# A mixture of experts in two parts of padded rows, with its results summed by TensorE through diagonal matrices

## The reference, cut to what matters

```python
logits = xt @ router_w.T                      # xt: 4096 x 128, router_w: 8 x 128
topk_vals, topk_idx = jax.lax.top_k(logits, 2)
g = jax.nn.sigmoid(topk_vals)
g = g / (g.sum(axis=-1, keepdims=True) + 1e-10)
# every chosen expert e of a token: (silu(x @ w_gate[e]) * (x @ w_up[e])) @ w_down[e]
```

## Time and profile before

| what | value |
|---|---|
| median of three runs | 2016.98 us (2016.55 to 2017.09) |
| the profiled execution | 2013.99 us |
| its span, first to last instruction | 2012.2 us |
| PE, DVE, ACT, POOL busy, share of the span | 85%, 76%, 68%, 44% |
| mean granted clock of TensorE | 0.923 |
| start of the mixture of experts | about 1727 us |

### The profile page before, as it was taken

How to read it: one execution, slowest core, us unless ns; L and a number is a source line. 1 busy time by engine, 2 the same in 40 slices (tenths; PEclk the granted TensorE clock), 3 DMA queues, 4 the chain that set the end, 5 groups by cost and what they waited for, 6 DMA issues and landing times. The chain is left out here.

```text
span 2012.2 us, 39279 instructions
## 1 busy us (share of the span) xinstructions
PE 1715.0 (85%) x12410; PEld 1129.4 (56%) x12410; DVE 1527.1 (76%) x4148; ACT 1360.3 (68%) x4708; POOL 883.9 (44%) x824
## 2 busy tenths in 40 slices
PE   4999999999999974899999696899999696744991
PEld 2555555555555542677777453677777453543660
DVE  2898898988889875899999455799999484753445
ACT  2888888888888854688888432688888455322555
POOL 3555565555565544333333123233333153385554
PEclk9999999999999985899999898899999898655996
DMA  6990000000000000000000110000000110012225
GB/s 201 214 179 2 2 2 2 2 1 2 1 2 1 2 1 6 6 17 17 12 17 12 26 32 7 6 17 16 13 17 12 26 32 2 8 46 70 82 64 135
DMA packets 102525, 65.90 MB, mean 33 GB/s; under 512 B 27698, under 2 KB 93874, under 8 KB 102322
## 3 DMA queue, kind: packets, MB, share of 16 engines
q1 hardware_dynamic: 97970, 54.40, 12.6%
q0 software_dynamic: 4352, 8.99, 1.3%
HBM read 19.50 MB, written 30.24 MB: 25 GB/s over the span
## 5 line engine op out<-in xcount | busy, mean ns | idle before, releaser
L216 POOL TENSOR_SCALAR a_aT<-a_dT 128x384 f32<-128x384 f32 x256 | 309.4, 1208 | 299.1 <-PE a_psO L529 187.5
L411 ACT ACTIVATE a_E<-a_psS,a_nm 128x128 f32<-128x128 f32 (+1 forms) x1028 | 418.8, 428 | 31.3 <-DVE a_nm L245 28.9
L245 DVE TENSOR_REDUCE a_nm<-a_psS 128x2 f32<-128x256 f32 (+1 forms) x514 | 260.1, 547 | 43.6 <-PE a_psS L496 42.9
L492 PE MATMUL a_psS<-a_kT,a_qm 32*128 32x128 f32 (+1 forms) x2064 | 240.6, 351 | 5.6 <-issue 3.6
L270 DVE SCALAR_TENSOR_TENSOR a_d<-a_E,a_cf 128x128 f32<-128x128 f32 (+1 forms) x512 | 219.3, 468 | 27.9 <-DVE a_cf L259 1.4
L411 ACT ACTIVATION_READ_ACCUMULATOR a_E<-a_psS,a_nm 128x1 f32 x1028 | 219.8, 214 | 0.0
L788 POOL TENSOR_TENSOR b0rn<-b0ss,minus_half 128x16 f32<-128x16 f32 x36 | 107.1, 2976 | 224.0 <-DVE b0ss L824 224.0
L788 POOL TENSOR_TENSOR b1rn<-b1ss,minus_half 128x16 f32<-128x16 f32 x36 | 107.1, 2976 | 221.5 <-DVE b1ss L824 221.5
L420 ACT ACTIVATE a_dT<-a_psT 128x384 f32<-128x384 f32 x256 | 126.7, 495 | 74.3 <-PE a_psT L505 71.3
L492 PEld LDWEIGHTS a_psS<-a_kT,a_qm 32*128 32x128 f32 x2064 | 136.6, 186 | 55.8 <-issue 35.5
L505 PE MATMUL a_psT<-ident,a_d 128*128 128x128 f32 x768 | 132.4, 281 | 6.2 <-DVE a_d L270 0.3
(11 more groups left out here) (353 smaller groups left out, 4411.9 us busy)
## 6 DMA issues: line engine op xcount, KB each, us to landing
mx_rows<-mx_blank SPq DMA_DIRECT2D x9, 2080.0 KB, 27.4
mx_xin<-mx_rows SPq DMA_DIRECT2D x72, 65.0 KB
b0v<-b0v SPq DMA_DIRECT2D x34, 128.0 KB, 2.3
b1v<-b1v SPq DMA_DIRECT2D x34, 128.0 KB
F<-mx_results SPq DMA_DIRECT2D x8, 256.0 KB, 5.2
mx_second<-mx_results SPq DMA_DIRECT2D x8, 256.0 KB, 5.4
out_dram<-X SPq DMA_DIRECT2D x8, 256.0 KB, 2.3
f0z<-F SPq DMA_DIRECT2D x9, 128.0 KB
```

Of the source, the lines that this page charges most:

```text
L216: pool.tensor_scalar(aT[:, s, :], dT[:, s, :], 0.0, None, ALU.max).then_inc(positived.sem, 1)
L245: ins = dve.tensor_reduce(nm[:, s, t, :], psS[:, s, :, (0, P)[t]:(P, 384)[t]], axis=AX.X, op=ALU.max, negate=True)
L411: ins = act.activation(E[:, s, m, c0:c1], psS[:, s, m, c0:c1], ACT.Exp, bias=nm[:, s, t, m:m + 1], accum_out=Z[:, p, h, t, m:m + 1])
L492: pe.matmul(psS[:, s, m, c0:c1], qm[rows, p, a, r, t * P:(t + 1) * P], kT[rows, p, a, 0:c1 - c0], start=(t == 0), stop=False)
```

## The change

- The groups are in two parts: groups 0 to 4 are the first, groups 5 to 7 the second. Each part has table regions, counts and a list of its own. Since each part needs up to eight half-filled tiles, there are 48 + 32 = 80 slots instead of 72.
- The slots of the first part start when its own sends are done. The last 12 sends (half of group 6 and all of group 7) are put one by one between the slots' scatters on POOL. The last group's routing, ranks and list lie between slots on PE and DVE: `route(7)` at slot 1, `choose(7)` at slot 3, `ranks(7)` at slot 6, `place(7)` at slot 8, the second list at slots 10 to 14.
- A row of the table has 144 numbers instead of 130. The ring of results `y` has 8 buffers instead of 4. `psH` has one bank instead of two, and the router's and the ranks' results share one bank.
- At the end ACT's and DVE's weighting is gone. DVE makes, for every tile, two diagonal matrices `ident * sg` (`spread`), those of the first part between slots 18 and 37, those of the second during the end. PE multiplies each tile's two results by them and sums both in PSUM. Statistics and norm read that PSUM tile; DVE adds the residual instead of POOL.

```diff
-ROW = D + 2
+ROW = D + 16
-SLOTS = 2 * TILES + NE
+FIRST = (0, 5, GROUPS)
+PART_TILES = [NT * (FIRST[p + 1] - FIRST[p]) for p in range(2)]
+PART_SLOTS = [2 * n + NE for n in PART_TILES]
+START = [0, PART_SLOTS[0], sum(PART_SLOTS)]
+SLOTS = START[2]
...
+                    if i == START[part]:
+                        sp.wait_ge(sent[part], 16 * 2 * PART_TILES[part])
...
+                    load(i)
+                    if i == START[1] + RING + 2:
+                        fetch(0)
+            fetch(1)
...
+            def spread(t):
+                dve.tensor_scalar(firsts[:, t, :], ident[:, :], sg[:, t, 0:1], None, ALU.mult)
+                dve.tensor_scalar(seconds[:, t, :], ident[:, :], sg[:, t, 1:2], None, ALU.mult).then_inc(diagonal, 1)
...
+            gates(0)
+            choose(LATE - 1)
+            place(LATE - 1)
+            outer.shifts(dve, LATE)
...
+            for g in range(GROUPS + 2):
                 if g < GROUPS:
-                    dve.wait_ge(weighted, g + 1)
...
                     dve.wait_ge(summed, g + 1)
                     ln.statistics(dve, g)
-                if g >= 1:
+                if 1 <= g <= GROUPS:
                     ln.shifts(dve, g - 1)
+                if g >= 2:
+                    dve.wait_ge(normal, g - 1)
+                    dve.tensor_tensor(ln.tiles(X, g - 2), ln.tiles(X, g - 2), second[:, of(g - 2), :], ALU.add)\
+                       .then_inc(done, 1)
+                if g == 0:
+                    gates(1)
...
+                if 1 <= g <= GROUPS - FIRST[1]:
+                    for t in range(NT):
+                        spread(NT * (FIRST[1] + g - 1) + t)
...
+            for g in range(GROUPS):
+                ln.apply(act, g, second[:, of(g), :]).then_inc(normal, 1)
...
+            pe.wait_ge(y_ready, SLOTS)
+            for g in range(GROUPS):
+                pe.wait_ge(diagonal, NT * (g + 1))
+                pe.wait_ge(fetched[g], 32)
+                if g >= 2:
+                    pe.wait_ge(normal, g - 1)
+                for t in range(NT):
+                    z = psY[:, g % 2, t * P:(t + 1) * P]
+                    pe.matmul(z, firsts[:, g * NT + t, :], ln.tiles(F, g)[:, t, :], start=True, stop=False)
+                    ins = pe.matmul(z, seconds[:, g * NT + t, :], second[:, g * NT + t, :], start=False, stop=True)
+                ins.then_inc(summed, 1)
```

More of the change, by code:

```diff
@@ L1589, in mixture_of_experts @@
         fetched = [sem(f"fetched{g}") for g in range(GROUPS)]
-        weighted, summed, normal, done, stored = (sem(n) for n in ("weighted", "summed", "normal", "done", "stored"))
+        diagonal, summed, normal, done, stored = (sem(n) for n in ("diagonal", "summed", "normal", "done", "stored"))
+        ln.sums = psY
         block = ctx.enter_context(nc.Block())
@@ L1604, in _ @@
         def _(sp):
[L1605 to L1617, removed]
@@ L1619, in _, with load @@
-            for k in range(4):
-                sp.wait_ge(scattered[k], 16 * (SLOTS // 4))
-            o = out.rearrange("b (t p) d -> p (b t) d", p=P)
-            for g in range(GROUPS):
[L1623 to L1627, removed]
+            def load(i):
+                sp.dma_start(xin[:, i % RING, :], rows[bass.ds(at[i], P), :]).then_inc(landed[i % RING], 16)
@@ new lines, in fetch, with store @@
+            def fetch(part):
+                for k in range(YR):
+                    sp.wait_ge(scattered[k], 16 * (START[part + 1] // YR))
+                for g in range(FIRST[part], FIRST[part + 1]):
+                    sp.dma_start(ln.tiles(F, g), result(0, g)).then_inc(fetched[g], 16)
+                    sp.dma_start(second[:, of(g), :], result(1, g)).then_inc(fetched[g], 16)
+            def store(g, ready, count):
+                sp.wait_ge(ready, count)
+                sp.dma_start(o[:, of(g), :], ln.tiles(X, g)).then_inc(stored, 16)
@@ L1635, in send, with send_group @@
                 pool.sem_inc(held, 1)
[L1636 to L1640, removed]
+            def send(g, n):
+                t, choice = divmod(n, 2)
+                pool.indirect_dma_start(
+                    rows, bass.IndirectOffsetOnAxis(ap=posu[:, g, choice, t:t + 1], axis=0),
+                    pay[:, g * NT + t, :], None).then_inc(sent[part_of(g)], 16)
+            def send_group(g):
+                ready(g)
+                for n in range(2 * NT):
+                    send(g, n)
             for g in range(LEAD):
@@ L1648, in _ @@
             pool.wait_ge(filled, 16 * fills)
-            for g in range(GROUPS):
-                send(g)
+            for g in range(LATE - 1):
+                send_group(g)
                 if g + 4 < GROUPS:
@@ L1654, in _ @@
                     outer.power(pool, g + 3)
+            ready(LATE - 1)
+            for n in range(NT):
+                send(LATE - 1, n)
             for i in range(SLOTS):
@@ L2030, in _ @@
             ranks(0)
-            for g in range(GROUPS):
+            for g in range(FIRST[1]):
                 if g + 4 < GROUPS:
```

303 lines of the change are left out of this document (180 added, 123 removed).

## The result

| | before | after |
|---|---|---|
| median | 2016.76 us (4 runs, 2015.07 to 2017.09) | 2049.12 us (4 runs, 2044.22 to 2055.62) |
| profiled execution, its span | 2013.99, 2012.2 us | 2048.01, 2046.2 us |
| mean granted clock of TensorE | 0.923 | 0.928 |

The changed kernel is slower, by a ratio of 1.0165 with a 95% interval of 1.0142 to 1.0187. The forecast had the sign, but 2049 lies outside its range (2015 to 2040).

What follows compares the result with a forecast made beforehand. It took POOL to bound the routing, PE the slots and DVE the end. Start and slots -7.0 plus end +18.4 made +11.4 us, a span of 2023.6; the forecast was 2028, range 2015 to 2040.

Steps and rivals of the forecast that it cites:

- the sign: Whole kernel: slower, by 0.56%; chance of slower 0.76.
- The start: Start of the slots: first gate_up 25.3 us earlier, at 1821.6, held by turn(7) behind place(6); bounds 22 and 30.6.
- the rival of an early start: Start and slots: shifts(7) doesn't hold the first slot, DVE's extra work is absorbed; -14.3 instead of -7.0; chance 0.06.
- The slots: Slots: eight more +12.9 us, PE's route, ranks and count +3.4, DVE's lateness +2.0; diagonals and POOL's sends at nothing.
- The rival of diagonals beside sends: Slots: diagonal products on DVE and POOL's sends collide, 4 to 6 us more, 2033; chance 0.14.
- The end: After the last result: sum, statistics, shift, norm in series, 7.4 us a group at half clock from group 2; +18.4 us.
- The rival of full clock throughout: End: clock stays at 2.4 GHz, so the end adds 6.1 us; 2016, not slower; chance 0.18.

Runs made afterwards that it cites:

- pauses behind the sends of groups 5 and 6: Changed kernel with four PSUM banks in the end and a 128x256 memset on POOL behind each scatter, late send and send of groups 5 and 6: 2012.33 us, 0.9991.
- the four banks: Changed kernel with the sums of the end in four PSUM banks (psY and psG in turn) instead of two: 2020.44 us, 1.0027 to the kernel before.
- the end alone: Kernel before with only the new end: 32 pairs of diagonals in slots 18 to 49, sums on PE in four banks, addition on DVE: 2005.45 us, 0.9959.
- The extra products: Kernel before with the new end, plus 28 products of 128 columns on PE that nobody reads, in the wait for the fetch: 2004.36 us, 0.9955.

## Why the prediction was half right

**The start: right but for waits that it didn't know.** `turn(7)` stood behind `place(6)` as said. The 4.9 us too late are 1.8 ahead of the transposes, by DVE's late start in `choose(6)`, and 3.2 between the transposes and ACT; the 3.6 to the first result are late starts of the same kind. They vary from one execution to the next: with nothing changed ahead of the slots the wait in `choose(6)` was 0.5 to 1.2 us in seven others, the first gate_up stood at 70.6 to 72.9 and the first result at 82.7 to 84.8. Only with pauses behind the sends of groups 5 and 6 were both lags of ACT 0.1 us or less and the first result at 79.8. One bound of this part was added up wrongly: the fortieth send against the last gives 1840.69 + 1.00 - 1810.30 = 31.4, not 30.6; only the rival of an early start rests on it.

**The slots: this step failed.** It said of POOL's four issues in three slots that it "falls 2.3 us behind, against a ring of eight results (12.9 us), so this is nothing too". The count of issues was right and POOL did not bind. What was missing is the cost of the twelve sends themselves to the other engines: with them ACT and DVE start up to 4.2 us behind PE's products. Each late result seems to bunch the ones behind it, so that POOL again issues without a pause; this is my reading of the timeline, not tested. 20 of the 24.8 us are this (16 to 17 by the other executions): taking the twelve sends out gives them back, putting twelve into the kernel before costs 18.8, twelve memsets or plain DMAs cost 3 us or less. The sum around it holds: without the sends first to last result is 132.9 us, forecast 133.1 with `route`, `ranks` and DVE's extra work, whose single terms no run measured.

A row of before showed it. Timeline of PE and DVE in the routing, while POOL sent:

```profile
1822.78 0.61 PE L1976 MATMUL mx_psY<-mx_seen,mx_ones 128*128 128x32 f32 x2
...
1826.61 0.19 DVE L1727 TENSOR_TENSOR mx_rank<-mx_psY,mx_region 128x32 f32<-128x32 f32 x1 [4.76 <-issue]
```

DVE starts 3.2 us behind the product that it waits for. In the routing POOL is the bound: it sends on with 0.30 us between the sends until 1840.69, so DVE's late start costs nothing there. In slots that PE bounds it can.

**The rival of diagonals beside sends** was right to suspect the sends and wrong on the place: the diagonals took 0.28 us each at the median, and moving them changed nothing that can be told. The GPSIMD Engine Reference of the Trainium skill, Key points, on the interfaces that GpSimd and VectorE share, does not explain the whole: ACT waits as well, and a memset on POOL costs 2.6 us where the sends cost 19.

**The end: right.** Sum, statistics, shift and norm follow each other; five periods from 1996.86 to 2030.55 are 6.74 us each, forecast 7.4, and the end 57.6 instead of 61.6. The period was over-sized, and it was luck that this took 4.0 off the miss: from the first product to the statistics it is 3.26 us (2003.52 to 2006.78, part of it at full clock) instead of 3.9, and statistics with the shift are 1.61 (to 2008.39) instead of 1.82; the norm's 1.65 was right. That the clock falls there was right, though it was not at half throughout: 0.51, 0.71 and 0.50 in the three stretches from 2004 on. TensorE: Matmul & The Clock Gate of the Trainium skill, Part 1, says that the clock is set by how busy the array has been recently; both ends agree in direction, 0.50 with PE at 3.96 of 8 us, 1.00 in the four banks with 7.21 of 8 and then 5.29 of 8. The rival of full clock throughout did not come to pass. I had not asked how much the chain was worth: with four banks the end is 24.1 us shorter.

## What to carry to other kernels

Where an engine starts microseconds behind a product that had ended, and the releaser is "issue", "remote" or a DMA of another stage, count the indirect DMAs that POOL issues there and look how close together they are: here POOL was half idle by its share, and twelve more indirect DMAs among 72 cost PE 16 to 19 us. When a reduction moves to another engine, count the banks between a group's first step and the reuse of its bank: with two, four engines stood in series here, with four they overlapped. Run the parts of a change alone: here the end alone gained 8 us on the kernel before, and the sends between the slots lost 16 to 20.

## What the hardware showed that I had not expected

- Indirect DMAs each 1.26 or 1.46 us: twelve added to the 72 of the slots cost 16 to 19 us. Each 1.67 us: 3 us, but then only 71 of the 84 fall in the slots. Twelve plain ones instead: 0.4 us. The bytes in a row (512, 520, 576) made no difference that could be told.
- Mostly it is what PE hands to ACT and DVE that comes late, by up to 4.2 us, often about 1 us behind POOL's last issue but at the start in the midst of its sends. Once it was DVE's own step (2.13 us in `choose(6)`), so it isn't PE alone. By which path the indirect DMAs hold this up stays open: the traces show no busy engine there.
- With PE idle from 1970 to 1974, TensorE's granted clock was 0.58 on the mean; with PE full from 1976 on it was still 0.50 until 1980, then 0.78, and 1.00 from 1982. The extra products that kept it up throughout saved nothing that the measurement can tell.
